# A graph attention kernel on one core: its last step ordered apart, with own places, GpSimd residuals and a second DMA queue

## What is computed

```python
# layer 0
q, k, v = x @ Wq + bq, x @ Wk + bk, x @ Wv + bv        # 8 heads of 64
a = softmax(q k^T / 8, masked by adj) v
x = layernorm(x + a @ Wo + bo)
# layer 1: the same without Wo and bo
x = layernorm(x + a)
```

## Time and profile before

| | us |
|---|---|
| median of 3 runs | 2998.36 (2998.1 to 2999.74) |
| the profiled execution | 2996.24 |
| its span, first to last instruction | 2994.4 |
| mean granted TensorE clock | 0.993 |
| TensorE busy (matmuls) | 2939.3 (98%) |
| VectorE, ScalarE, GpSimd busy | 1815.3 (61%), 1495.2 (50%), 1358.2 (45%) |

### The profile page before, as it was taken

How to read it: one execution, slowest core, us unless ns; L and a number is a source line. 1 busy time by engine, 2 the same in 40 slices (tenths; PEclk the granted TensorE clock), 3 DMA queues, 4 the chain that set the end, 5 groups by cost and what they waited for, 6 DMA issues and landing times.

```text
span 2994.4 us, 58006 instructions
## 1 busy us (share of the span) xinstructions
PE 2939.3 (98%) x18956; PEld 2478.4 (83%) x18956; DVE 1815.3 (61%) x7060; ACT 1495.2 (50%) x5007; POOL 1358.2 (45%) x1285
## 2 busy tenths in 40 slices
PE   7999999999999999999999999999999999999996
PEld 5888888888888888888888788888888888888885
DVE  3565656566555656465656666666766666676665
ACT  4444445454545444444545455555555555555552
POOL 2445545455555554554545534334434333443442
PEclk9999999999999999999999999999999999999997
DMA  5344453534344444444354445556555555655555
GB/s 188 89 123 131 114 141 106 148 106 134 110 132 113 135 117 124 131 115 140 107 148 141 131 132 161 160 167 169 147 144 155 161 159 167 170 150 142 155 161 156
DMA packets 411007, 417.70 MB, mean 139 GB/s; under 512 B 46112, under 2 KB 308512, under 8 KB 410656
## 3 DMA queue, kind: packets, MB, share of 16 engines
q1 hardware_dynamic: 409408, 413.32, 49.3%
q10 hardware_dynamic: 1296, 0.67, 0.1%
HBM read 145.37 MB, written 103.81 MB: 83 GB/s over the span
## 4 chain that ended last, share of the span: by engine, by line
PE 95%; issue 1%; ACT 1%; DVE 1%; SPq 1%; DMA 1%; POOL 0%; POOLq 0%; DVEq 0%; ACTq 0%
PE ring L330 46%; PE ring L338 34%; PE ring L362 8%; PE ring L373 7%; ACT prob L489 1%; SPq L233 0%; DMA prob<-w_k 0%; DMA x_raw<-x_feat 0%; DVE prob L578 0%; SPq L227 0%; SPq L244 0%; POOL norm L746 0%; POOL xt_lo L729 0%; DVE w_lo_k L547 0%; DVE w_lo_o L541 0%
## 5 line engine op out<-in xcount | busy, mean ns | idle before, releaser
L489 ACT ACTIVATE prob<-prob,neg_max 128x128 f32<-128x128 f32 x2048 | 792.1, 393 | 114.4 <-DVE neg_max L578 114.4
L739 POOL TENSOR_TENSOR prob<-prob,inv_sum 128x512 f32<-128x512 f32 x512 | 538.1, 1077 | 591.7 <-DVE inv_sum L586 591.5
L469 ACT ACTIVATE k_all<-ring,bk_col 128x512 f32<-128x512 f32 x256 | 311.7, 1217 | 690.0 <-PE ring L330 690.0
L578 DVE CUSTOM_DVE_ANT_0 prob<-ring,mask 128x128 f32<-128x128 f32 x2048 | 440.7, 284 | 312.2 <-PE ring L362 312.0
L729 POOL TENSOR_TENSOR xt_lo<-x_raw,xt_hi 128x512 fp32r<-128x512 f32 x196 | 261.6, 1346 | 444.9 <-DVE xt_hi L553 444.9
L476 ACT ACTIVATE q_all<-ring,bq_col 128x512 f32<-128x512 f32 x256 | 176.5, 689 | 486.4 <-PE ring L330 486.4
L338 PE MATMUL ring<-w_hi_v,xt_hi 128*128 128x512 f32 x1024 | 406.9, 397 | 8.3 <-DVE neg_max L578 8.3
L330 PE MATMUL ring<-xt_hi,w_hi_k 128*128 128x512 f32 x1024 | 399.4, 390 | 13.5 <-DVE w_lo_k L541 13.5
L338 PE MATMUL ring<-w_hi_v,xt_lo 128*128 128x512 f32 x1024 | 399.4, 390 | 0.0
L330 PE MATMUL ring<-xt_lo,w_hi_k 128*128 128x512 f32 x1024 | 399.3, 390 | 0.0
L338 PE MATMUL ring<-w_lo_v,xt_hi 128*128 128x512 f32 x1024 | 399.1, 390 | 0.0
(11 more groups left out here) (67 smaller groups left out, 4720.1 us busy)
## 6 DMA issues: line engine op xcount, KB each, us to landing
prob_t<-turned SPq DMA_DIRECT2D x1024, 128.0 KB, 2.7
x_res<-x_tok SPq DMA_DIRECT2D x256, 256.0 KB, 3.7
x_raw<-x_feat SPq DMA_DIRECT2D x196, 256.0 KB, 3.3
x_feat<-x_turned SPq DMA_DIRECT2D x512, 64.0 KB, 2.1
x_tok<-x_bias SPq DMA_DIRECT2D x128, 256.0 KB, 2.3
at_lo<-x_bias SPq DMA_DIRECT2D x256, 64.0 KB, 2.1
at_lo<-x_turned SPq DMA_DIRECT2D x256, 64.0 KB, 2.1
out<-x_bias SPq DMA_DIRECT2D x64, 256.0 KB, 4.2
```

Source lines behind the costliest of these rows:

```text
L469: act.activation(k_all[:, m, :].rearrange("p (b j n) -> p b n j", b=QB, n=SQ), ring[K_BANK[m]][:].rearrange("p (b n j) -> p b n j", b=QB, ...
L489: last = act.activation(prob[b][:, i, n, :], prob[b][:, i, n, :], ACT.Exp, bias=neg_max[b][:, i, n:n + 1], scale=-1.0, accum_out=row_sum[b ...
L578: last = dve.tensor_tensor_reduce(prob[b][:, i, n, :], score_bank(b, i)[:, n, :], mask[layer][:], -SCALE, BIG, ALU.add, ALU.min, neg_max[b ...
L739: pool.tensor_tensor(prob[b][:, i], prob[b][:, i], inv_sum[b][:, i, :].unsqueeze(2).to_broadcast([P, NC, NODES]), ALU.mult).then_inc(norm_ ...
```

## The change

Steps 0 to 62 stay as they are; step 63 and what follows get lists of their own.

- TensorE: `attend` of quad 62's graphs 0 to 2 ahead of the third query; graph 3 behind the scores. Values 1 to 3 then wait for the masks of the fifth, sixth and seventh half. Queries of step 63 go to banks 0, 1, 5, 6; attentions of quad 62 to 2, 3, 4, 0, of quad 63 to 1, 2, 3, 7.
- Places of quad 63: residual rows in `k_all`, turned probabilities of graphs 2 and 3 in `prob[0]` and `prob[1]`, attentions turned into `x_raw` and `x1`, carried into `q_all`.
- VectorE: one list, `end_of_program`. GpSimd: the residuals of graphs 2 and 3 of quad 62 and 0 and 1 of quad 63.
- DMAs: ScalarE issues carry 62/3 (quad 62, graph 3), carry 63/2 and six stores, behind its last copy of step 63; SyncE the rest.

```diff
+        def query_bank(s, m):
+            return [0, 1, 5, 6][m] if s == LAST else m
+
+        def att_bank(a, b):
+            if a == LAST:
+                return [1, 2, 3, 7][b]
+            return [2, 3, 4, 0][b] if a == LAST - 1 else b
+
...
-            return t[:].rearrange("p n (e c q) -> p e c n q", e=2, c=NC)
+            return t.rearrange("p n (e c q) -> p e c n q", e=2, c=NC)
...
+        def blocks1(a, b):
+            return (x_raw + x1)[b] if a == LAST else (x1_bias + x1_turned)[b]
+
+        def res_of(a, b):
+            return k_all[:, b, :] if a == LAST else x_res[b][:]
+
+        def turned_of(a, b):
+            if a == LAST and b >= 2:
+                return prob[b - 2][:].rearrange("p a c n -> p (a c n)").rearrange("p (n k) -> p n k", n=BLK)
+            return turned[b % 2][:]
+
+        def attention_turned(a, b):
+            rows = q_all[:, b, :] if a == LAST else at_lo[b][:].rearrange("p c n -> p (c n)").bitcast(F32)
+            return rows.rearrange("p (r c f) -> p r c f", r=BLK, c=NC)
+
+        def carry_attention(eng, a, b):
+
+            if a == LAST:
+                eng.wait_ge(score_done, 2 * QB * (LAST + 1))
+            else:
+                eng.wait_ge(sum_set, QB * a + b - 3)
+            eng.wait_ge(at1_blocks_set, QB * (a - G) + b + 1)
+            for n in range(BLK):
+                eng.dma_start(attention_turned(a, b)[:, n].rearrange("p c f -> p (c f)"),
+                              blocks1(a, b)[n * SQ:(n + 1) * SQ].rearrange("p (n k) -> p n k", n=BLK)
+                              ).then_inc(at1_in[b], 16)
+
+        def store_y(eng, a, b):
+            eng.wait_ge(ln_set, QB * a + b + 1)
+            eng.dma_start(out[a - G, b], blocks1(a, b)[:]).then_inc(y_out[b], 16)

         block = ctx.enter_context(nc.Block())
...
             def load_res(a, b):
-                need(sp, ln_set, QB * a + b - 3)
+                if a == LAST:
+                    sp.wait_ge(score_done, 2 * QB * (LAST + 1))
+                else:
+                    need(sp, ln_set, QB * a + b - 3)
                 if a < G:
                     src = x_tok[a, b]
                 else:
                     src = x1_tok[a - G, b]
                     sp.wait_ge(x1_tok_out[b % 2], 16 * (2 * (a - G) + b // 2 + 1))
-                sp.dma_start(x_res[b][:], src).then_inc(x_in[b], 16)
+                sp.dma_start(res_of(a, b), src).then_inc(x_in[b], 16)

             def turn_probs(a, b):
                 need(sp, att_done, QB * a + b - 3)
                 sp.wait_ge(turned_set, 2 * (QB * a + b) + 2)
                 for n in range(BLK):
-                    sp.dma_start(prob_t[b][:, n], turned[b % 2][n * SQ:(n + 1) * SQ]).then_inc(prob_t_in[b], 16)
+                    sp.dma_start(prob_t[b][:, n], turned_of(a, b)[n * SQ:(n + 1) * SQ]).then_inc(prob_t_in[b], 16)

...
                 if layer_of(f) == 0:
                     store_x1(f, b)
                 else:
-                    store_y(f, b)
-                if f + 1 <= LAST:
+                    store_y(sp, f, b)
+                if f + 1 < LAST:
                     load_res(f + 1, b)
...
+                if s == LAST:
+                    for b in range(3):
+                        carry_attention(sp, a, b)
+                    for b in range(QB):
+                        load_res(LAST, b)
+                    turn_probs(LAST, 0)
+                    turn_probs(LAST, 1)
+                    turn_probs(LAST, 2)
+                    turn_probs(LAST, 3)
+                    carry_attention(sp, LAST, 0)
+                    carry_attention(sp, LAST, 1)
+                    carry_attention(sp, LAST, 3)
+                    store_y(sp, LAST, 0)
+                    store_y(sp, LAST, 2)
+                    return
                 if la == 1:
-                    carry_attention(a, 0)
...
-                        last = pe.matmul(ring[b][e * HD:(e + 1) * HD, c * NODES:(c + 1) * NODES],
-                                         v_of(a, b)[:, h * HD:(h + 1) * HD], by_head(prob_t[b])[:, e, c],
+                        last = pe.matmul(ring[att_bank(a, b)][e * HD:(e + 1) * HD, c * NODES:(c + 1) * NODES],
+                                         v_of(a, b)[:, h * HD:(h + 1) * HD], by_head(prob_t[b][:])[:, e, c],
                                          start=True, stop=True)
                 last.then_inc(att_done, 1)
...
+                        if s == LAST and m == 2:
+
+                            pe.wait_ge(at1_blocks_set, QB * (s - 1 - G))
+                            pe.wait_ge(k_set, NC * s + NC)
+                            for b in range(3):
+                                attend(a, b)
                         queries(s, m)
...
                     scores(s, 0)
+                    if s == LAST:
+                        pe.wait_ge(at1_blocks_set, QB * (a - G) + 3)
                     scores(s, 1)
                     scores(s, 2)
                     pe.wait_ge(v_set, QB * s + 1)
                     scores(s, 3)
-                if la is not None:
-                    for b in range(QB):
-
-                        if lp is not None:
+                    if s == LAST:
+                        pe.wait_ge(masked_set, 2 * QB * s + 1)
+                        attend(a, 3)
+                    elif la is not None:
+                        for b in range(QB):
+
                             pe.wait_ge(masked_set, 2 * QB * s + b + 1)
-                        else:
-                            pe.wait_ge(at1_blocks_set, QB * (a - 1 - G) + b + 1)
-                        attend(a, b)
-                if lp is not None:
+                            attend(a, b)
                     for b in range(1, QB):

                         pe.wait_ge(masked_set, 2 * QB * s + 4 + b)
                         values(s, b)
+                else:
+                    pe.wait_ge(masked_set, 2 * QB * s)
+                    for b in range(QB):
+                        attend(a, b)
                 if first:
...
             for i in range(4):
                 first_high(i)
             act.wait_ge(small_in, 16 * 9)
-            for s in range(2 * G + 1):
+            for s in range(2 * G):
                 step(s)
+            carry_attention(act, LAST - 1, 3)
+            store_y(act, LAST - 1, 0)
+            store_y(act, LAST - 1, 1)
+            carry_attention(act, LAST, 2)
+            store_y(act, LAST - 1, 2)
+            store_y(act, LAST - 1, 3)
+            store_y(act, LAST, 1)
+            store_y(act, LAST, 3)

...
-                if b >= 2:
+                if a == LAST and b >= 2:
+                    dve.wait_ge(turned_set, 2 * (QB * a + b) - 2)
+                elif b >= 2:
                     dve.wait_ge(prob_t_in[b - 2], 64 * (a + 1))
...
             def turn_attention(a, b):
                 dve.wait_ge(att_done, QB * a + b + 1)
-                if a > G:
+                if a == LAST:
+                    dve.wait_ge(x_lo_set, QB * (a + 1))
+                elif a > G:
                     dve.wait_ge(y_out[b], 16 * (a - G))
...
-                dve.transpose(blocks1[b][:].rearrange("p (n c f) -> p c n f", n=BLK, c=NC),
-                              ring[b][:].rearrange("p (c q n) -> p c n q", c=NC, n=BLK)).then_inc(at1_blocks_set, 1)
+                dve.transpose(blocks1(a, b)[:].rearrange("p (n c f) -> p c n f", n=BLK, c=NC),
+                              ring[att_bank(a, b)][:].rearrange("p (c q n) -> p c n q", c=NC, n=BLK)).then_inc(at1_blocks_set, 1)
...
-            def statistics(a, b):
+                total = res_of(a, b).rearrange("p (c r f) -> p r c f", c=NC, r=BLK)
+                dve.tensor_tensor(total, attention_turned(a, b), total, ALU.add).then_inc(sum_set, 1)
+
+            def statistics(a, b, summed, value):
                 done = QB * a + b + 1
-                dve.wait_ge(sum_set, done)
-                dve.bn_stats(stats[b], x_res[b][:]).then_inc(stats_set, 1)
+                dve.wait_ge(summed, value)
+                dve.bn_stats(stats[b], res_of(a, b)).then_inc(stats_set, 1)
...
                 normalise(f, b)
                 if layer_of(f) == 0:
                     turn_x1(f, b)
+
+            def end_of_program():
+
+                a = LAST - 1
+                turn_attention(a, 0)
+                turn_attention(a, 1)
+                turn_attention(a, 2)
+                finish_start(a, 0)
+                for b in range(3):
+                    mask_scores(LAST, b, 1)
+                invert_sums(LAST, 0)
+                mask_scores(LAST, 3, 1)
+                invert_sums(LAST, 1)
+                finish_end(a, 0)
+                turn_blocks(LAST, 0)
+                turn_attention(a, 3)
+                invert_sums(LAST, 2)
+                turn_blocks(LAST, 1)
+                finish_start(a, 1)
+                invert_sums(LAST, 3)
+                turn_blocks(LAST, 2)
+                finish_end(a, 1)
+                turn_blocks(LAST, 3)
+                turn_attention(LAST, 0)
```

(47 more changed lines are left out.)

34 lines of the change are left out of this document (10 added, 24 removed).

## The result

Twelve runs of the changed kernel gave a median of 2990.88 us (2989.39 to 2993.33), twelve of the kernel before beside them 2998.76 (2996.24 to 3000.14): a ratio of 0.9976, 95% interval 0.9968 to 0.9984, so 7.2 us less, with the interval from 4.8 to 9.6 (the two medians lie 7.9 apart). The forecast was 2991.0, 7.4 less.

The account below looks back on a forecast made before the run. After step 63 begins, SyncE's DMA issuing sets the pace; +1.6 us at the last exponentials, -5.2 at the last turned probabilities, the rest from unqueued carries and transposes: -7.4 off the 2998.36 median gives 2991.0, range 2988.5 to 2994.8.

Parts of the forecast that it names:

- Steps 1 to 5: From step 63 on: early attentions and carries, key-tile loads, VectorE's list; last exponentials +1.6 us, last turned probabilities -5.2.
- Step 6: Quad 63's own places: its turned probabilities and attentions wait for no earlier landing or store; a transpose waited up to 2.27 us.
- Step 7: Four residuals (0.72 us each) leave VectorE for GpSimd at 1.28 us an add; its waiting holds back 62/3's inverse deviation.
- the new late item: GpSimd's inverse deviation of 62/3, sum ready by 2966, held behind the add of 63/0 until 2973.6.
- The rule weighed in the prediction: VectorE and GpSimd exclude each other on a shared port pair; collisions about 1 and 0.7 us, 0.35 reaching the end.
- Step 8: ScalarE's second queue takes carries 62/3, 63/2 and quad 62's stores, some 7 us of issues, off SyncE.
- Step 9: VectorE's last statistics and normalisations run serially to 2984.5, then a store of 2.48 us; span 2987.0.
- Case B: Collisions and crowded landings, chance 0.18: probabilities 0.5 us later, carry 63/0 1.3, collisions 1 more; 2.8 in all, 2993.8.
- Case C: SyncE was never the bound, chance 0.04: only the two waits for stores go, 3 us; 2995.4.
- Case D: Slower, chance 0.04: transfers on ScalarE's queue land late; decides from 6.6 us, at 8.7 gives 3004.7 by the median.
- signs of being wrong: ScalarE's carries landing over 4 us, VectorE gap before masks, add over 1.6, 63/3's probabilities issued after 2967, span over 2990.
- step 3: Quad 62's early carries on SyncE: VectorE's residual and statistics of 62/0 end at 2942.8, 2.6 us ahead of the masks.

## Why the prediction was right, and where it was not

The forecast of 2991.0 rests on a chain of placed instructions, and most of its places are found in the trace. As times from step 63's first matmul (forecast, its base taken off, then measured): masks 28.6, 28.9; values 1 at 32.9, 33.2; last exponentials' end 42.9, 43.1; last probabilities turned 48.0, 47.7; GpSimd's add of 63/0 54.9, 55.8; normalise 62/3 56.8, 57.6; end of the last normalisation 67.7, 68.3; end of the span 70.2, 70.9.

*Steps 1 to 5* (attentions moved, TensorE's added wait, early carries) hold. The added wait was 0.80 us; the price at the exponentials was 1.8 for 1.6. Without the early attentions the tail is 2.5 us longer.

*Step 6* (own places) holds: without them the tail is 2.3 us longer.

*Step 7* (GpSimd residuals): the price was right, 1.26 for 1.28. But I called the inverse deviation held back behind the add of 63/0 "the new late item". It stands on the chain of waits that I followed, VectorE idle for 4.0 us, and yet the way without it was 1.4 us slower. The wait kept a 256 KB store out of the landing of a carry; that was luck, not part of the forecast. The four residuals moved are worth nothing sure once the stores are late: four of 0.72 less on VectorE, and 0.3 gained. The rule weighed in the prediction (SBUF — State Buffer, "SBUF: two separate sides", of the Trainium skill), by which they are worth less than their count, points the same way, but these tails do not show that the lock is the reason: three of the four adds took 1.26 us without a collision, and VectorE stood idle before their results.

*Step 8* (second queue) named 7 us of issues that leave SyncE, and the weighing of the rule said that the measurement speaks for more than the skill does. That was too strong: with one queue the tail is 71.1, the same. What I left out is that issues grow while large stores are on their way (6.44 for 5.09 in the changed kernel), and that the order of the stores counts for as much as the queue. In that comparison the stores moved too; with late stores on both sides two queues are 1.2 to 1.5 us ahead, so the second queue is not shown to be worth nothing either. The Trainium skill (DMA: Bandwidth & Descriptors, "Issuing engines are not separate DMA queues") says that all of it ends on the same 16 engines and only issue time is saved; the equal tails do not contradict that. That the issue is usually small beside the transfer is not what these traces show for carries: 2.5 us of some 4.2.

*Step 9* holds in each duration. The 0.7 us that the tail is longer than forecast came in ahead of it, at the carry of 63/0: the issues of 63/2 and 63/3 took 6.44 instead of 5.1 (done at t = 51.2, forecast 50.6). Their probabilities landed after a median of 3.5 us instead of 2.8, which stayed hidden behind GpSimd. The stores of 62/0 and 62/1, which the forecast let leave without a price, were issued beside them. That the total came within 0.2 us of the median is partly luck: by the tails the change brought 6.7 and 6.2 us where I had 7.4, and the timed interval is 4.8 us wide.

*Case B* was a matter of landings and collisions, and both are in the trace. Collisions lengthened the normalisation of 62/0 (1.28 for 0.55), the residual of 62/1 (1.48 for 0.69) and one add (1.71 for 1.26); I had 1 and 0.7 for the first two and nothing for the third. The probabilities landed 0.7 late, more than B's 0.5. But at the end of the tail only 0.7 of B's 2.8 us arrived. *Case C* falls: the early carries and the places each gave over 2 us. *Case D* falls: four 64 KB pieces on ScalarE's queue landed after a median of 3.0 us (carry 62/3) and 2.3 us (carry 63/2). Two of the signs of being wrong that I had named came all the same: one add of over 1.6 us (1.71), which shows a collision that I had not priced, and a gap of VectorE ahead of the masks (2.56 us), which is the slack of step 3 (2.6) and speaks against nothing.

Taken singly, the early attentions (2.5) and the places (2.3) make 4.8 of the 6.5 us. They need not add up in that way, since each was taken out of the changed kernel alone. The rest, among it the residual rows' own place and SyncE's changed order, was not taken apart.

## What to carry to other kernels

At the end of a pipeline, list what each DMA queue still has to issue and move what depends on nothing new into the stretch where the matrix engine still has work, even at a small price on the path. Give the last block places of its own: the tiles that a next block would have filled are free. And once the path runs over small transfers, hold back the large stores that nobody waits for: a wait that looks idle may be what keeps them apart. To judge a second queue, leave the order of the stores as it is.

## What the runs showed that I had not expected

- ScalarE's DMA instructions did not wait for its arithmetic ahead of them: carry 62/3 was issued at 2960.26, with a value copy ahead of it in the program that started only at 2961.57. They did wait for what that copy waits for: TensorE's last value matmul ended at 2960.16. That is t = 41.8; I had placed the carry behind the copy, at 43.6 (2960.4 - 2916.8).
- Issues slow down while many transfers are on their way: 0.60 us each on SyncE in the usual case, eight in 7.16 us with ScalarE's issues and two stores beside them. A second queue that issues at the same moment is not needed for it: with late stores and the residuals on VectorE, one issue of SyncE at 2971.35 took 1.47 us, while the next on ScalarE's queue came at 2974.06. Nor is it enough: ScalarE's 2.52 us above were beside SyncE's issues. Which limit is behind it stays open.
- TensorE's clock fell later in the tail than in the kernel before, where 63/0 too was at half speed (1.97 us). The attentions of quad 63 in TensorE's timeline of the changed kernel:

```profile
2962.01 1.09 PE L413 MATMUL ring<-prob_t,v_first 128*64 128x128 f32 x16 [1.85 <-issue]
...
2969.26 1.98 PE L413 MATMUL ring<-prob_t,v_other 128*64 128x128 f32 x16 [2.29 <-DMA prob_t<-prob]
2972.92 1.97 PE L413 MATMUL ring<-prob_t,v_other 128*64 128x128 f32 x16 [1.68 <-DMA prob_t<-prob]
```

And the windows of two stretches (the granted clock is the number behind the fifth engine's count):

```profile
2960.00:2965.00 5.00, 1.26 (x17) 0.88 (x16) 3.62 (x10) 2.16 (x11) 4.15 (x4) 1.00 0.87 210
2968.00:2976.00 8.00, 3.95 (x32) 3.15 (x32) 2.54 (x6) 0.00 (x0) 2.09 (x3) 0.50 0.73 181
```

The attention of 63/0, after 1.85 us without work, still took 1.09 us at a granted clock of 1.00, 2.4 GHz; those of 63/2 and 63/3 took 1.98 and 1.97 at 0.50, 1.2 GHz. For 63/3 I had the low clock and 1.97 us. It changed nothing here: 63/3's ended at 2974.89, and VectorE, next in line for it, stood until 2976.00 for GpSimd.
